# Route stage of a two-layer attention and mixture-of-experts kernel: small loads and output copies moved into the attention, the halves' splitting re-spread, sums on TensorE

## The reference

```python
x = x + L0_xattn(layernorm(x), ctx, ...)
x = x + L0_ffn(layernorm(x), ...)
x = x + L1_xattn(layernorm(x), ctx, ...)
x = x + L1_ffn(layernorm(x), Wr, br, W1, b1, W2, b2)

# L1_ffn
scores = einsum('bsd,de->bse', x, Wr) + br
_, topk_idx = top_k(scores, 2)
weights = softmax(where(indicator > 0, scores, -inf))
for i in range(8):
    h = relu(einsum('bsd,dh->bsh', xi, W1[i]) + b1[i])
    out = out + (einsum('bsh,hd->bsd', h, W2[i]) + b2[i]) * weights[..., i:i + 1]
```

## Time and profile before

| | |
|---|---|
| time, median of 3 runs | 1535.91 us (1535.61 to 1539.75) |
| the profiled execution | 1535.06 us, its span in the profile 1532.9 us |
| TensorE busy | 1277.0 us, 83% of the span |
| VectorE busy | 1052.7 us, 69% |
| ScalarE busy | 819.9 us, 53% |
| GpSimd busy | 521.5 us, 34% |
| second attention | 711 to about 951 us |
| `route` | 955 to 1083 us |
| `experts` | from 1083 us to the end |

### The profile page before, as it was taken

One profiled execution on the slowest core, in us unless ns is written; L12 is line 12 of the kernel. 1 busy time (PEld: TensorE's weight loads), 2 busy tenths in 40 slices (PEclk: granted clock), 3 DMA queues, 4 the chain that ended last, 5 costly groups with the idle time before them and its releaser, 6 DMA issues. The chain is left out here.

```text
span 1532.9 us, 29296 instructions
## 1 busy us (share of the span) xinstructions
PE 1277.0 (83%) x8839; PEld 969.9 (63%) x8840; DVE 1052.7 (69%) x2032; ACT 819.9 (53%) x1209; POOL 521.5 (34%) x430
## 2 busy tenths in 40 slices
PE   7779999959984839897899996642599999999996
PEld 3446766734431638764567675542499898989895
DVE  4859999775699775655688887655265656666653
ACT  3655555465698787415777785532243434343432
POOL 2066776500000000000777674476032233322333
PEclk9899999979998559958999999555799999999998
DMA  5010000000144762001132211853232222222220
GB/s 211 26 41 1 0 0 0 1 1 0 42 164 167 251 214 83 1 1 45 30 96 68 92 59 57 293 182 109 88 53 47 45 42 51 40 49 44 49 39 9
DMA packets 63214, 106.87 MB, mean 70 GB/s; under 512 B 9713, under 2 KB 50769, under 8 KB 62001
## 3 DMA queue, kind: packets, MB, share of 16 engines
q1 hardware_dynamic: 48848, 89.17, 17.8%
q0 software_dynamic: 14304, 16.93, 6.2%
HBM read 67.89 MB, written 40.01 MB: 70 GB/s over the span
## 5 line engine op out<-in xcount | busy, mean ns | idle before, releaser
L2101 POOL DMA_INDIRECT out<-ex_yo,ex_mt x78 | 130.6, 1674 | 325.3 <-DVE ex_yo L2076 186.9
L2020 ACT ACTIVATE ex_hT<-ex_ps_h,e_b1T,e_unscale 128x256 f32<-128x256 f32 x312 | 150.5, 563 | 115.5 <-PE ex_ps_h L1978 115.5
L1978 PE MATMUL ex_ps_h<-ex_xT_hi,a_arena 128*128 128x256 f16 x1248 | 211.9, 273 | 0.2 <-issue 0.2
L674 PE MATMUL at_ps_s<-a_arena,at_xnT_hi 128*128 (+1 forms) x512 | 160.8, 397 | 33.4 <-issue 23.6
L696 PE MATMUL at_ps_y<-c_VW,at_pT_hi 128*128 (+1 forms) x1024 | 171.1, 273 | 1.3 <-DVE main_x_res L823 1.3
L1978 PE MATMUL ex_ps_h<-ex_xT_lo,a_arena 128*128 128x256 f16 x624 | 170.7, 274 | 0.0
L1991 PE MATMUL ex_ps_y<-a_arena,ex_hT_lo 128*128 x624 | 170.1, 273 | 0.0
L1991 PE MATMUL ex_ps_y<-a_arena,ex_hT_hi 128*128 x624 | 170.1, 273 | 0.0
L1991 PE MATMUL ex_ps_y<-e_w_lo,ex_hT_hi 128*128 x624 | 170.1, 273 | 0.0
L945 POOL TENSOR_TENSOR at_sc<-at_sc,at_ri 128x960 f32<-128x960 f32 (+1 forms) x96 | 132.0, 1389 | 84.4 <-DVE at_ri L818 84.1
L1187 PE MATMUL gm_bank<-f_xq,f_wide 128*128 (+1 forms) x576 | 129.7, 385 | 20.7 <-ACT gm_stg L1225 16.2
(11 more groups left out here) (321 smaller groups left out, 2876.1 us busy)
## 6 DMA issues: line engine op xcount, KB each, us to landing
at_half<-in_L_ffn_W SPq DMA_DIRECT2D x32, 512.0 KB, 4.3
up_scratch<-gm_stg SPq DMA_DIRECT2D x16, 768.0 KB, 3.2
gm_stg<-up_scratch SPq DMA_DIRECT2D x16, 768.0 KB, 4.3
ex_row<-xs SPq DMA_DIRECT2D x39, 260.0 KB, 2.7
rt_stage<-in_L_ffn_W SPq DMA_DIRECT2D x16, 512.0 KB
main_x_res<-in_x SPq DMA_DIRECT2D x8, 512.0 KB, 12.0
out<-main_x_res SPq DMA_DIRECT2D x4, 1024.0 KB, 12.6
xs<-rt_pad SPq DMA_DIRECT2D x18, 130.0 KB
```

Source lines behind the costliest of these rows:

```text
L674: last = nc.tensor.matmul(ps_s[j][:, c * CH:(c + 1) * CH], a[:, d, :], b[:, d, bass.ds(off + c * CH, CH)], start=(n == 0), stop=(n == 3 * ...
L1978: last = nc.tensor.matmul(ps_h[:, n, :], a[:, bass.ds(e * WN + d * HID + n * P, P)], b[:, d, :], start=(m == 0), stop=(m == 3 * DT - 1))
L2020: last = nc.scalar.activation(hT[:, n, :], ps_h[:, n, :], ACT.Relu, bias=b1T[:, bass.ds(e * HT + n, 1)], scale=unscale[:, 0, bass.ds(e, 1)])
L2101: nc.gpsimd.indirect_dma_start(out=acc[:, :], out_offset=bass.IndirectOffsetOnAxis(ap=mt[j][:, q, 1:2].bitcast(U32), axis=0), in_=yo[j][:, ...
```

## The change

Five things are changed, all of them around `route`:

1. The three small loads of the router (`b1r`, `wr`, `brb`) are issued in the second attention, behind the first halves. For this SP's loop over the experts is written out.
2. The copy of `x_res` to the output is cut into eight parts of four tiles each (512 KB). Seven leave in the attention, as soon as their tiles are final; the last one leaves in `route` behind the first four halves.
3. The maximum over partitions on GpSimd becomes a sum over partitions by a matmul with ones on TensorE (behind `turn(1)`), and a copy on VectorE. As an upper bound of the magnitude a sum serves as well as the maximum.
4. The halves are spread anew. `HIGHS` has a tuple for each group: none in group 0, two in the groups 1 to 5 (tiles 1 and 3 of the group), three in the groups 6 and 7 (tiles 0, 1 and 3). `high` now stands behind `ratio` in the same tile. The `low`s of a group's halves stand behind `place` of that group, those of group 7 behind the table.
5. Eleven small operations that make the scales for `experts` (`inner_scales`) stand behind `place(0)`.

```diff
@@ attention, SP
                 load_half(1, 0, 1)
+                for dst, src in ahead["loads"]:
+                    sp.dma_start(dst, src).then_inc(ahead["in"], 16)
                 for sem in used:
                     sp.sem_clear(sem)
-                with nc.sync.Fori(1, E, 1) as e:
+                for e in range(1, E):
...
                     sp.wait_ge(ssq_r, 4 * e + 1)
                     load_half(1, e, 1)
+                    sp.wait_ge(res_r, 4 * e)
+                    ahead["copy"](sp, e - 1)
@@ route
-    HIGHS = (2, 3)
+    HIGHS = ((),) + 5 * ((1, 3),) + 2 * ((0, 1, 3),)
...
+        def highs_to(c):
+
+            return sum(len(h) for h in HIGHS[:c])
@@ route, SP
-            sp.dma_start(b1r[:, :], w["L1_ffn_b1"].rearrange("e (t p) -> (e t) p", p=P)).then_inc(r_in, 16)
-            sp.dma_start(wr[:, :, :], w["L1_ffn_Wr"].rearrange("(t p) e -> p t e", p=P)).then_inc(r_in, 16)
-            sp.dma_start(brb[:, :], w["L1_ffn_br"].unsqueeze(0).to_broadcast([P, E])).then_inc(r_in, 16)
...
             for q in range(NS):
                 load_half(q)
-            for g in range(B):
-                sp.dma_start(acc[g * S:(g + 1) * S, :].rearrange("(p t) d -> p t d", p=P),
-                             x_res[:, g * NT // B:(g + 1) * NT // B, :]).then_inc(acc_in, 16)
+            router["copy"](sp, E - 1)
             for q in range(NS, 2 * E):
                 load_half(q)
@@ route, GpSimd
-            pool.wait_ge(bm_r, 1)
-            g.partition_all_reduce(bmr[:, :, :], bm[:, :, :], P, RMAX).then_inc(bmr_r, 1)
@@ route, TensorE
             for t in range(NT):
                 turn(t)
+                if t == 1:
+                    pe.wait_ge(cst, CONSTS)
+                    pe.wait_ge(bm_r, 1)
+                    nc.tensor.matmul(ps_c[1][:, 0:2 * E], ones[:, :], bm[:, :, :], start=True, stop=True).then_inc(sum_r, 1)
@@ route, ScalarE
                 copy(t)
-                if t == 2:
+                c, i = divmod(t, TK)
+                if t == TK:
                     act.wait_ge(wsc_r, 1)
-                if t % TK in HIGHS:
-                    high(2 * (t // TK) + HIGHS.index(t % TK))
                 if t % TK == 1 and t > TK:
                     ratio(t // TK - 1)
+                if i in HIGHS[c]:
+                    high(highs_to(c) + HIGHS[c].index(i))
@@ route, VectorE
+            dve.wait_ge(sum_r, 1)
+            v.tensor_copy(bmr[:, :, :], ps_c[1][:, 0:2 * E].rearrange("p (k e) -> p k e", k=2)).then_inc(bmr_r, 1)
...
-            lows(0, 2)
             for m in range(NK):
                 choose(m)
                 place(m)
+                if m == 0:
+                    inner_scales()
                 if m < NK - 1:
-                    lows(2 * m + 2, 2 * m + 4)
+                    lows(highs_to(m), highs_to(m + 1))
...
             v.tensor_scalar(table[:, 1, :], tf[:, 1, :], float(E - 1), None, ALU.min)
+            lows(highs_to(NK - 1), highs_to(NK))
@@ program
+                def copy_rows(sp, i):
+
+                    g, h = divmod(i, 2)
+                    half = slice(4 * h, 4 * h + 4)
+                    sp.dma_start(acc[g * S:(g + 1) * S, :].rearrange("(p t) d -> p t d", p=P)[:, half, :],
+                                 x_res[:, 4 * i:4 * i + 4, :]).then_inc(acc_in, 16)
```

More of the change, by code:

```diff
@@ L567, in attention @@
 def attention(nc, tag, groups, bias_in, x_res, mv, rstd, nmr, stats, ident, M, VW, unscale, experts_w=None, ssq=None, w1=None, totals=None,
-              quant=None, used=()):
+              quant=None, used=(), ahead=None):
     assert NT == 4 * E
@@ L1563, in _, with route @@
                         last.then_inc(mm, 1)
-def route(nc, w, b1T, eid, x_res, rstd, nmr, ident, w2, ssq, sums, unscale, xs, acc, table):
+def route(nc, w, router, b1T, eid, x_res, rstd, nmr, ident, w2, ssq, sums, unscale, xs, acc, table):
     TK = 4
@@ L1685, in _ @@
             for j in range(NB * TK):
-                pool.wait_ge(sent[j], 32 * NT // (NB * TK))
+                pool.wait_ge(sent[j], 32 * len(range(j, NT, NB * TK)))
         @block.tensor
@@ L2126, in program, with cross @@
                                "v_down", "v_up", "v_alpha", "o_down", "o_up", "o_alpha")))}
-        def cross(layer, weights, groups, bias, M, arena=None, quant=None, fold=None, w1=None, sums=None, used=()):
+        def cross(layer, weights, groups, bias, M, arena=None, quant=None, fold=None, w1=None, sums=None, used=(), ahead=None):
             with Scope(nc, f"c{layer}") as z:
@@ L2138, in cross @@
                 attention(nc, f"at{layer}", groups, bias, x_res, mv, rstd, nmr, stats, ident, M, VW, unscale,
-                          (w["L1_ffn_W1"], w["L1_ffn_W2"]) if layer else None, ssq, w1, sums, quant, used)
+                          (w["L1_ffn_W1"], w["L1_ffn_W2"]) if layer else None, ssq, w1, sums, quant, used, ahead)
         with Scope(nc, "a") as a:
@@ L2183, in program @@
                 xs = nc.dram_tensor("xs", (E * CAP + TR, ROW), F32, kind="Internal").ap()
-                acc = out.rearrange("b s d -> (b s) d")
                 rstd_of(nc, "r4", stats, mv, rstd, nmr)
-                route(nc, w, b1T, eid, x_res, rstd, nmr, ident, w2, ssq, sums, unscale, xs, acc, table)
+                route(nc, w, router, b1T, eid, x_res, rstd, nmr, ident, w2, ssq, sums, unscale, xs, acc, table)
                 experts(nc, w["L1_ffn_b2"], b1T, eid, x_res, w1, w2, unscale, ident, xs, acc, table)
```

54 lines of the change are left out of this document (30 added, 24 removed).

## The result

The changed kernel takes 1526.19 us (median of 20 executions, 1519.84 to 1544.63), the kernel before 1536.14 (20 executions, 1530.93 to 1540.92). The ratio is 0.9946, with a 95% interval of 0.9923 to 0.9970: faster by 0.54%, some 8 to 10 us. My likeliest case, "no change that can be measured", was wrong; the range 1525.5 to 1543.0 holds the value, 0.7 us from its lower end.

The account below looks back on a forecast made before the run. Route was taken as a chain of waits, its end hanging on scatters and counts. Counts: −7.6 + 1.2 + 16.9 − 7.6 = +2.9 us; stage end 0.1 us earlier, 1535.9 − 0.1, taken as 1535.5 us; range 1525.5 to 1543.0.

Parts of the forecast that it names:

- no change that can be measured: Whole kernel: the likeliest case, a difference within about 0.3% (4.6 us); chance 0.43.
- The sum: Whole kernel: counts +2.9 us, stage end 1083.2 instead of 1083.3, so 1535.9 − 0.1, taken as 1535.5 us.
- The head: Start of route: choose(0) at about 962.0 instead of 969.91, choose(1) at 970.8 instead of 978.47, −7.6 us.
- The loads of the halves: Groups 5, 6 and ahead of choose(7) in route: ScalarE's high waits for loads, +4.4, +6.5 and +6.0, together +16.9 us.
- Late semaphores: VectorE's groups in route: of 20.2 us of stalls, group 5's 7.6 counted as replaced by the new waits, −7.6 us.
- The tail: End of route: SP's pads start at 1061.5, three of eight experts slow, stage end at 1083.2 where it was 1083.3.
- Sums on TensorE: Head of route: the all-reduce and its 4.40 us wait go; a matmul and a copy of 0.3 us come, hidden.
- the halves don't wait: Rival, route: loads arrive in time, counts 6.4 us earlier, late semaphores stay, −7.2 us to 1528.7; chance 0.25.
- the late semaphores go: Rival, route: the late semaphores vanish as well, stage ends at 1070 to 1073, time 1523 to 1526 us; chance 0.10.

Follow-up runs that it names:

- after: The profiled execution of the changed kernel from its first measurement, one of the four long ones: 1544.63 us, median of the 20 executions 1526.19 us.
- after_2: The changed kernel, unchanged, measured again beside the kernel before: 1521.88 us, ratio 0.9894.
- copies_back: The changed kernel with all eight copies of x_res issued in route behind the first four halves, none in the attention: 1509.16 us, ratio 0.9912 to the kernel before.
- before_2: The kernel before, unchanged, one more execution for its profile: 1537.97 us.
- lows_lead: The changed kernel with each group's low operations one group earlier: 1518.42 us, ratio 0.9882 to the kernel before; run again 1517.90 us, 0.9861.
- second group: Four variants on one chip (copies in route, old spread of halves, scatters bounded, scatters spaced): ratios 0.9912, 0.9921, 1.0015, 0.9972; the kernel before took 1523.71 us there.

## Why the prediction was right or wrong

The number lies in the range, and partly by luck. The sum, 1535.5 us, was 9.3 us too high, the likeliest case failed, and the four long executions help to keep the median above 1525.5: the other sixteen have 1525.2, outside. Two steps failed, the tail and the start of the program.

**The head: right.** Predicted for `choose(0)` R+6.8 and `choose(1)` R+15.6; measured 6.7 and 15.2. The first scatter came at R+13.3.

**The loads of the halves: right in mechanism and place, a little too large.** Terms 4.4, 6.5 and 6.0 us; measured without late semaphores 2.8 (3.5 between the starts of `choose`), 4.9 and 5.7. ScalarE waited 27.4 us for stage loads, and `choose(7)` came 21.0 us behind `choose(6)`, predicted about 20. Where `high` waited for its load, it started 4.1 to 4.3 us behind the load's issue (halves 4, 6, 10, 12 and 14 in after, after_2 and copies_back; half 8 at 4.1, 5.4 and 5.7), so the landing I had taken holds, and what was too large is what I put behind it. The fit of the Trainium skill's page "DMA: Bandwidth & Descriptors", section "Anatomy of one DMA — SWDGE (gpsimd) path", is one of DMAs that GpSimd issues; these loads are issued by SP, and the 3.2 us by that fit are not seen in any of them.

**Late semaphores: the term was a guess, and near by luck.** I let group 5's go; it stayed (6.85 us), and group 4's went. Against copies_back, in which VectorE has the same order and nothing is late, the counts of the two profiles of the changed kernel are 16.6 and 12.9 us late, of which 12.9 and 8.2 are such waits; my sum left 12.6 of 20.2. (Of those 20.2 us the profile of before names 14.1 as "remote"; that all of it is of this kind I had assumed.) The counts were 4.5 us later than before, predicted 2.9.

**The tail: wrong by 4 us.** The step that failed is "SP starts at 1061.5, makes three of eight experts in the slow stretch". The scatters ended about where I had them (issue R+115.5, predicted 114.6), but SP made no expert in a slow stretch, and the pads were not what the stage waited for. I predicted the end 0.1 us earlier than before; the first load of `experts` came 3.9 us earlier, and in after_2, against before_2, 9.5 us. I had taken SP's slow steps for an effect of scatters under way. That alone doesn't make them: in copies_back the last eight scatters and the pads run side by side, and the pads take 13.2 us. What does is open. The five profiles with slow pads have late semaphores, the copies in `route`, and counts that came 8 to 17 us into an unbroken train; in the changed kernel's two the counts come within half a microsecond of the train's new start, and the copies have left in the attention. No run parts these conditions, as copies_back ran where nothing is late.

**The start of the program: not in the prediction at all.** It is the step "*Sums on TensorE.* The all-reduce and its 4.40 us wait go". I priced the removed operation where it stood, and put nothing for the next execution, where its absence is worth 4.7 us. The wait of 9.56 us at the beginning of the page stood in the profile of before, marked "issue" like the 7.42 us of the earlier trace rows, and I didn't ask what it was. It is paid by the next execution for what this one leaves on GpSimd. The three profiles with an all-reduce last start late, all others early, and a single unused all-reduce moves the kernel from the one to the other.

**The sum.** −4.7 us at the start, and −3.9 (first pair of profiles) or −9.5 (second pair) in `route`, where I had −0.1, make −8.6 to −14.2; measured −8 to −10 and −16 us. The rival "the halves don't wait" had its time for another reason, and of "the late semaphores go" something is in the second pair. What I had not seen either: where nothing is late, the waits for loads lie under the scatters, and the whole head's gain of 8.0 us can reach the end. 4.7 + 8.0 is 12.7 us, and copies_back measured 0.9912, 13.4 us; for the kernel before on that chip this is an inference, as it has no profile there.

**Which edit did it.** The sum on TensorE alone gives 0.9932. The small loads, the copies and the empty group 0 bring the first scatter from R+18.3 to R+13.3. Where semaphores are late, the re-spread behind it gives some of that back in waits, as lows_lead shows: 0.9946 and 0.9894 for the whole. With the lows a group earlier it is 0.9882 and 0.9861.

## What to carry to other kernels

An operation on GpSimd that needs other code than its neighbours costs a change there and one back, and the one back can stand at the start of the next execution: look at the first microseconds of the profile for a wait marked "issue", and leave GpSimd at the end with what the beginning wants. Where one engine issues a fixed train (64 scatters at 1.28 us) and ends the stage, ask when it starts and whether it pauses; what comes earlier beside it was worth nothing here, with counts 11.7 us earlier in a stage that ended later. When a schedule is re-spread over few buffers, count for each buffer how far apart its release and its next use are: shifting the releases back by one group was worth 5 to 7 us where semaphores come late.

## What the runs showed of the hardware that was not expected

- **An early start sometimes meets a slow TensorE.** In the kernels whose affine_select stands at 1.5 us, 19 of 114 executions were 12 us or more above their median; in those with it at 10.5 to 10.7, none of 96. Two of the 19 have a profile. Both show the 64 matmuls of line 201 at 0.56 to 0.59 us from start to start, where all others change to 0.31 to 0.32 after at most four, and the first four of line 209 at 0.79 to 1.01 where the rest stands at 0.43. That is nearly the factor of two between TensorE's clock levels, 1.2 and 2.4 GHz. The row of the granted clock reads 1.00 all the same (window 0 to 50 us), but only for want of a record: the first clock record in the trace, one of full clock, begins at 49.8 and 50.3 us in these two, where the matmuls become fast, and at 9.9 to 16.8 us in the other twelve. TensorE was busy the whole time from 10 us on; why the full clock came so late is open. At some 18 us for one in six, about 3 us of the 4.7 are lost again in the mean.
- **Late semaphores come and go between groups of runs.** In the second group none of four kernels had one, and the kernel before was 12 us faster there; in the others every profile has 8 us or more of them on VectorE, at places that change from execution to execution. Each group had a chip and a time of its own, so that the chip is the cause is likely, but not shown. What makes them is still open.
- **GpSimd's change of code** has no busy row: 6.8 to 10.8 us of idle time marked "issue" ahead of the next operation. What gives it away is the `MODIFY_POOL_CONFIG` in the source view of that operation's line, which stands there also where it costs nothing.
